# Scanning the next batch's first two rows between the matmuls of fc2, loading look-ahead tokens at row 84, and moving the softplus bias to ScalarE

## The reference

```python
xz = h @ in_w;  xs, z = split(xz);  xs = silu(xs)
proj = xs @ xproj_w
dt = softplus(proj[..., :512] + dt_bias)
Bm, Cm = ...                                # 64 states each
hst = hst * exp(dt_t * A) + (dt_t * x_t) * B_t     # 512 steps in time
y_t = einsum('bds,bs->bd', hst, C_t)
...
ffn_out = gelu(x2 @ fc1_w.T + fc1_b) @ fc2_w.T + fc2_b
x = x + ffn_out * gamma2
```

## Time and profile before

| | |
|---|---|
| median of 3 runs | 3171.84 us (3170.88 to 3175.58) |
| profiled execution | 3174.25 us, its span 3172.5 us |
| PE / DVE / ACT / POOL busy | 98% / 87% / 85% / 78% of the span |
| rows 0 to 127 of batch 1, from its first scan | 852.1 to about 1469 us |
| fc2 between batches 0 and 1 | 837.5 to 851.3 us |

### The profile page before, as it was taken

One profiled execution on the slowest core, in us unless ns is written; L12 is line 12 of the kernel. 1 busy time (PEld: TensorE's weight loads), 2 busy tenths in 40 slices (PEclk: granted clock), 3 DMA queues, 4 the chain that ended last, 5 costly groups with the idle time before them and its releaser, 6 DMA issues.

```text
span 3172.5 us, 59515 instructions
## 1 busy us (share of the span) xinstructions
PE 3097.2 (98%) x23304; PEld 2631.1 (83%) x23304; DVE 2759.5 (87%) x3049; ACT 2703.8 (85%) x4496; POOL 2484.2 (78%) x638
## 2 busy tenths in 40 slices
PE   8999999999999999999999999999999999999999
PEld 6998899884699889988479988998848998888965
DVE  3999999977499999997659999999666999999963
ACT  3999999974699999995579999999558999999845
POOL 2999999971199999996139999999415999999910
PEclk9999999999999999999999999999999999999999
DMA  5222222210222232221022232223102223222100
GB/s 185 80 84 67 85 73 84 74 56 29 74 69 82 74 92 68 82 85 65 1 84 67 82 87 79 74 82 89 46 14 80 81 76 89 69 74 82 57 14 8
DMA packets 195240, 225.69 MB, mean 71 GB/s; under 512 B 77449, under 2 KB 149641, under 8 KB 193681
## 3 DMA queue, kind: packets, MB, share of 16 engines
q1 hardware_dynamic: 194960, 221.89, 22.8%
HBM read 217.37 MB, written 4.48 MB: 70 GB/s over the span
## 4 chain that ended last, share of the span: by engine, by line
PE 82%; POOL 8%; issue 4%; DVE 3%; ACT 1%; DMA 0%; SPq 0%; DVEq 0%; ACTq 0%; POOLq 0%
PE bank L1129 23%; PE bank L1109 17%; PE bank L1009 11%; PE bank L1110 10%; POOL states L674 5%; PE bank L1105 4%; PE bank L1353 4%; POOL y_gated L674 3%; PE bank L1390 2%; PE bank L1493 2%; PE bank L1378 2%; DVE states L1640 2%; PE bank L1184 1%; PE bank L1136 1%; PE bank L1281 1%
## 5 line engine op out<-in xcount | busy, mean ns | idle before, releaser
L674 POOL TENSOR_TENSOR states<-states,c_rows 128x2048 f32<-128x2048 f32 x336 | 1531.6, 4574 | 132.4 <-DVE states L1640 129.9
L1640 DVE TENSOR_TENSOR_SCAN states<-decay,bank 128x512 f32<-128x512 f32 x1376 | 1577.4, 1201 | 16.5 <-ACT decay L854 1.2
L854 ACT ACTIVATE decay<-dt,a_log 128x512 f32<-128x512 f32 x2048 | 1305.5, 710 | 0.0
L845 ACT ACTIVATE inflow_tok<-dtx_tok,b_tok 128x512 f32<-128x512 f32 x1536 | 995.7, 713 | 85.7 <-PE bank L1110 74.6
L1109 PE MATMUL bank<-ident,inflow_tok 128*128 128x128 f32 x5280 | 904.7, 280 | 35.8 <-DVE states L1640 18.7
L1129 PE MATMUL bank<-ident,states 128*128 128x128 f32 x5504 | 826.0, 273 | 6.1 <-DVE y_gated L1646 3.0
L1640 DVE TENSOR_TENSOR_SCAN y_gated<-decay,bank 128x512 f32<-128x512 f32 x672 | 777.1, 1202 | 14.0 <-ACT decay L854 5.0
L674 POOL TENSOR_TENSOR y_gated<-y_gated,c_rows 128x2048 f32<-128x2048 f32 x168 | 768.4, 4574 | 19.8 <-DVE y_gated L1640 18.1
L1109 PEld LDWEIGHTS bank<-ident,inflow_tok 128*128 128x128 f32 x5280 | 598.9, 141 | 205.7 <-issue 87.6
L1110 PE MATMUL bank<-b_diag,dtx_tok 128*128 128x128 f32 x3520 | 681.3, 275 | 0.0
L1129 PEld LDWEIGHTS bank<-ident,states 128*128 128x128 f32 x5504 | 645.0, 141 | 14.3 <-POOL states L674 7.8
(11 more groups left out here) (174 smaller groups left out, 2592.3 us busy)
## 6 DMA issues: line engine op xcount, KB each, us to landing
c_rows<-c_spill SPq DMA_DIRECT2D x256, 512.0 KB, 3.7
b_diag<-diag_ring SPq DMA_DIRECT2D x256, 128.0 KB, 2.3
xproj_w<-in_xproj_w SPq DMA_DIRECT2D x32, 320.0 KB, 3.8
in_w<-in_in_w SPq DMA_DIRECT2D x16, 512.0 KB, 4.5
out_w<-in_out_w SPq DMA_DIRECT2D x4, 1024.0 KB, 8.2
in_w<-in_fc_w SPq DMA_DIRECT2D x8, 512.0 KB, 4.3
xproj_w<-in_w SPq DMA_DIRECT2D x8, 512.0 KB, 4.7
xproj_w<-in_fc_w SPq DMA_DIRECT2D x4, 1024.0 KB, 4.7
```

What stands on the lines that cost most here:

```text
L674: pool.tensor_tensor(state_row, state_row, c_row.to_broadcast([P, KI, L]), ALU.mult).then_inc(weighed, PAIRS)
L845: last_tok = act.activation(inflow_tok[:, r % SLOTS, t, :], dtx_tok[:, d, t, :], ACT.Copy, scale=b_tok[:, d, t, s:s + 1])
L854: act.activation(decay[:, r % SLOTS * KI + k, :], dt[:, d, k, :], ACT.Exp, scale=a_neg[:, d, k, s:s + 1]).then_inc(decay_ready, 1)
L1640: dve.tensor_tensor_scan(state_slots[r % STATES][:, k, time], decay[:, slot, time], banks[k % INFLOW_BANKS][:, time], 0.0, ALU.mult, ALU.a ...
```

## The change

Three edits in one. (1) PE interleaves ten turns of the next batch (rows 0 and 1, and two tiles of row 2) into fc2, after its matmuls number 9, 12, ... 31 (0 to 31); DVE scans rows 0 and 1 there, ahead of the residual adds of tiles 1, 2 and 3. In the row loop those turns and scans are left out for b > 0. SP loads `b_diag` of rows 2 and 3 right after the C rows of the next batch, before fc1 ends. (2) `x_ahead` of batch b+2 is loaded at row 84 of batch b, in place of batch b+1 at row 0; only batch 1's stays at row 0 of batch 0. (3) ACT adds the bias in place in the PSUM guest bank (Identity with bias), and takes Exp straight from the bank; DVE's two half caps go, and the cap of 40 moves into the last DVE step, which now is min and then max.

```diff
+EARLY_AT = (9, 12, 15, 18, 21, 24, 27, 30, 31, 31)
+EARLY_SCANS = SLOTS * KI
-DT_CAP = 30.0
+DT_CAP = 40.0
-DT_CAP_AT = (30, 36, 40, 44)
-DT_CAP_REST_AT = (31, 37, 41, 45)
+DT_BIAS_AT = (31, 37, 41, 45)
+AHEAD_LOAD_AT = 84
@@ SP, batch
-                    if d == 0 and at == 0 and not last:
-                        sp.dma_start(x_ahead[:], x_rows[b + 1]).then_inc(ahead_loaded, 16)
+                    if r == 0 and b == 0:
+                        sp.dma_start(x_ahead[:], x_rows[1]).then_inc(ahead_loaded, 16)
+                    if r == AHEAD_LOAD_AT and b + 2 < B:
+                        sp.wait_ge(ahead_norm, (b + 2) * TT)
+                        sp.dma_start(x_ahead[:], x_rows[b + 2]).then_inc(ahead_loaded, 16)
-                    if not (last and r == BATCH_ROWS - HALF):
+                    if (r or not b) and not (last and r == BATCH_ROWS - HALF):
                         load_diag(b * BATCH_ROWS + r + HALF)
...
                     spread_rows(b + 1, HALF)
+                    load_diag((b + 1) * BATCH_ROWS + HALF)
                     sp.wait_ge(fc1_mm, (b + 1) * KF)
@@ ACT, prepare
+                if s in DT_BIAS_AT:
+                    k = DT_BIAS_AT.index(s)
+                    if k == 0:
+                        act.preload_act_table_set("natural_log_exp_and_others")
+                    act.wait_ge(dt_mm, n * KI + k + 1)
+                    act.activation(guest[(k + 1) % 2], guest[(k + 1) % 2], ACT.Identity,
+                                   bias=dt_b[:, d, k:k + 1]).then_inc(dt_biased, 1)
                 if s in DT_EXP_AT:
                     k = DT_EXP_AT.index(s)
-                    if k == 0:
-                        act.preload_act_table_set("natural_log_exp_and_others")
-                    act.wait_ge(dt_capped, n * KI + k + 1)
-                    act.activation(part[:, k, :], part[:, k, :], ACT.Exp).then_inc(dt_exp, 1)
+                    act.wait_ge(dt_biased, n * KI + k + 1)
+                    act.activation(part[:, k, :], guest[(k + 1) % 2], ACT.Exp).then_inc(dt_exp, 1)
@@ PE, scan_row and fc2
-                    turn_inflow(b, r, k)
+                    if not b or r * KI + k >= len(EARLY_AT):
+                        turn_inflow(b, r, k)
...
+                        for i, at in enumerate(EARLY_AT):
+                            if at == t * KF + c and b < B - 1:
+                                turn_inflow(b + 1, i // KI, i % KI)
@@ DVE, prepare, batch
-                        last = dve.scalar_tensor_tensor(dt[:, d, k, c], guest[(k + 1) % 2][:, c], dt_b[:, d, k:k + 1],
-                                                        part[:, k, c], ALU.add, ALU.max)
+                        last = dve.scalar_tensor_tensor(dt[:, d, k, c], part[:, k, c], DT_CAP, guest[(k + 1) % 2][:, c],
+                                                        ALU.min, ALU.max)
-                    if s in (DT_CAP_AT[k], DT_CAP_REST_AT[k]):
-                        ...
-                        last = dve.tensor_scalar(part[:, k, c], guest[(k + 1) % 2][:, c], dt_b[:, d, k:k + 1], DT_CAP,
-                                                 ALU.add, ALU.min)
+            def early_scans(b, t, last):
+                for i in range(EARLY_SCANS):
+                    if EARLY_AT[i] // KF == t and not last:
+                        scan_row(b + 1, i // KI, (i % KI,))
+                    early = b > 0 and r * KI < EARLY_SCANS
+                    if not early:
+                        scan_row(b, r, range(0, PAIR))
...
                 for t in range(TT):
+                    early_scans(b, t, last)
                     dve.wait_ge(res_mm, (b * RES + 3) * TT + t + 1)
                     dve.tensor_tensor(x_out[:, t, :], banks[OUT_BANK + t][:, 0:D], x_att[:, t, :], ALU.add).then_inc(out_ready, 1)
```

More of the change, by code:

```diff
@@ L331, in build @@
         dt_mm = sem("dt_mm")
-        dt_capped = sem("dt_capped")
+        dt_biased = sem("dt_biased")
         dt_exp = sem("dt_exp")
@@ L859, in _ @@
             for s in range(NS):
-                if s == DT_EXP_AT[0]:
+                if s == DT_BIAS_AT[0]:
                     act.wait_ge(ssm_loaded, 16 * len(SSM))
@@ L1492, in batch @@
                             pe.wait_ge(fc1_ready, b * KF + c + 1)
-                        last = pe.matmul(banks[OUT_BANK + t][:, 0:D], gelu_h[:, c, t * P:(t + 1) * P], fc2_w[:, c, :],
-                                         start=(c == 0), stop=(c == KF - 1))
-                    last.then_inc(res_mm, 1)
+                        last_mm = pe.matmul(banks[OUT_BANK + t][:, 0:D], gelu_h[:, c, t * P:(t + 1) * P], fc2_w[:, c, :],
+                                            start=(c == 0), stop=(c == KF - 1))
+                        if c == KF - 1:
+                            last_mm.then_inc(res_mm, 1)
+                        for i, at in enumerate(EARLY_AT):
+                            if at == t * KF + c and b < B - 1:
+                                turn_inflow(b + 1, i // KI, i % KI)
             for b in range(B):
@@ L1599, in prepare @@
                             dve.wait_ge(dt_log, n * KI + k + 1)
-                        last = dve.scalar_tensor_tensor(dt[:, d, k, c], guest[(k + 1) % 2][:, c], dt_b[:, d, k:k + 1],
-                                                        part[:, k, c], ALU.add, ALU.max)
+                        last = dve.scalar_tensor_tensor(dt[:, d, k, c], part[:, k, c], DT_CAP, guest[(k + 1) % 2][:, c],
+                                                        ALU.min, ALU.max)
                         if s == DT_READY_REST_AT[k]:
                             last.then_inc(dt_ready, 1)
-                    if s in (DT_CAP_AT[k], DT_CAP_REST_AT[k]):
-                        c = part_of(s, DT_CAP_AT[k], DT_CAP_REST_AT[k])
-                        if s == DT_CAP_AT[k]:
-                            dve.wait_ge(dt_mm, n * KI + k + 1)
-                        last = dve.tensor_scalar(part[:, k, c], guest[(k + 1) % 2][:, c], dt_b[:, d, k:k + 1], DT_CAP,
-                                                 ALU.add, ALU.min)
-                        if s == DT_CAP_REST_AT[k]:
-                            last.then_inc(dt_capped, 1)
             def look_ahead(b, s):
@@ L1657, in _ @@
                     dve.tensor_scalar(scale_cap[:], scale_mul[:], MAX_SCALE_MUL, None, ALU.min).then_inc(cap_ready, 1)
-                if s == DT_CAP_AT[0]:
-                    dve.wait_ge(ssm_loaded, 16 * len(SSM))
                 if s == DT_READY_AT[0]:
@@ L1670, in batch @@
                     d, s = r // NS, r % NS
-                    scan_row(b, r, range(0, PAIR))
+                    early = b > 0 and r * KI < EARLY_SCANS
+                    if not early:
+                        scan_row(b, r, range(0, PAIR))
                     if d == 0 or not last:
@@ L1683, in batch @@
                         gate_rows(b, 0)
-                    scan_row(b, r, range(PAIR, KI))
+                    if not early:
+                        scan_row(b, r, range(PAIR, KI))
                 r = BATCH_ROWS - 1
```

## The result

The changed kernel takes **3157.98 us** in the median of 4 runs (3156.91 to 3159.10), the kernel before 3173.71 in the 4 runs beside them: ratio **0.9949, 95% interval 0.9935 to 0.9964**, so 15.7 us faster by the medians. The profiled executions differ by 17.3 us (3174.25 to 3156.91). The forecast was 3152.0 with 3143 to 3166 around it: the time lies 6.0 us above the forecast and inside the range. Of these, 1.9 lie in the kernel before, whose median came out at 3173.71 where the forecast started from 3171.84; the gain itself is 15.7 us where 19.8 were forecast.

The account below looks back on a forecast made before the run. Four nearly full engines bound the rows (POOL paces direction 0, DVE direction 1), with bubbles ahead of batches 1 to 3. Early scans and loads 14.8, softplus 4.5, first preparation 0.5: 19.8 us off 3171.84 gives 3152.0 us, range 3143 to 3166.

Parts of the forecast that it names:

- fc2 and the early turns: Next batch's turns and scans inside fc2: fc2 ends 4.4 us later, turns 1.85 us apart, POOL's row 2 earlier.
- the tenth turn's wait: At fc2's end, PE's tenth turn must wait for the eighth scan, to 857.2 us.
- the 16.3: Gains up to POOL's row 2 in batches 1 to 3: 5.9, 7.1 and 3.3 us, before the store's loss.
- The loads' share: Part of the gain up to row 2 from moved loads: 2.6 us in batch 1, 3.8 in batch 2.
- Rival 2: Early turns in fc2 gain nothing, fc2 stretching as much as scans gain; only loads' 6.4 us left, 3165.4 us; chance 0.08.
- The output store: ACT waits for it ahead of row 4; landing in 6.0 us, it loses 1.5 us over batches 1 to 3.
- The lead of 2.2: ACT's decay of row 5 ready 2.2 us before its scan in batch 1, absorbing part of the store wait.
- Softplus: Seven preparations in the row loops: DVE loses 3.0 us each, ACT gains 2.4; gain 4.5 us, bounds 9 gained, 3 lost.
- The start: First preparation, ahead of batch 0's rows: shorter chains and an earlier table load, 0.5 us gained.
- the signs that would have made the prediction wrong: fc2 growing by more than 5 us, rows losing pace behind row 4, or DVE waiting for decay in softplus rows.
- Rival 1: ACT sets the first rows, row 4 waiting for the store: 8.6 us gained, softplus nothing, 3162.7 us; chance 0.17.
- Rivals 3 and 4: In softplus preparations: 3, ACT becomes the bound, 3180.3 us, chance 0.07; 4, Identity reloads tables, about 3240 us, chance 0.02.

Follow-up runs that it names:

- e5: Only the two load edits (x_ahead at row 84, b_diag of rows 2 and 3 before fc1's end) on the kernel before: 3168.75 us, ratio 0.9986.
- e1: The changed kernel with ACT's wait for the output store moved from ahead of row 4 to ahead of row 10: 3149.28 us, ratio 0.9921.
- e8: The changed kernel with one more ACT copy of 512 columns behind each softplus Identity: 3158.62 us, single run.
- e7: The changed kernel with two added DVE instructions of 256 columns per tile, both inputs in SBUF, in all preparations but the first: 3317.55 us, single run.
- e12: The changed kernel with DVE's removed softplus load put back behind the select, reading a PSUM bank and constants: 3166.63 us, ratio 0.9978.
- e4: The softplus edit alone on the kernel before: 3161.49 us, ratio 0.9960.
- e10: The changed kernel with the store wait at row 10 and the ten early turns spread more evenly over fc2: 3150.72 us, ratio 0.9927.
- e11: The changed kernel with the 512 KB load of x_in issued at row 10 in place of row 2: 3152.62 us, single run.
- e2: The changed kernel with SP issuing the output store ahead of the four xproj_w loads: 3150.43 us, ratio 0.9926.
- e9: The changed kernel with two more ACT copies of 512 columns behind each softplus Identity: 3167.21 us, single run.

## Why the prediction was right, and where not

1. **fc2 and the early turns: right.** fc2 18.4 us long (forecast 18.2), turns 1.85 apart, the eighth scan and the tenth turn's wait where they were put. POOL's row 2 came 25.4 us after fc2's first matmul in all three batches (861.08 - 835.67, and 25.4 twice more) against 25.0 forecast, so 5.5, 6.7 and 2.9 = 15.1 us of the 16.3. The table's marks show 16.5, since attention and MLP were 1.4 us shorter in this execution. The loads' share of it, 2.6 + 3.8, was 2.4 + 3.6 when done alone (e5, with the caution given there). Rival 2 is out.
2. **The output store: the mechanism was right, the size was not; this is the step that failed.** The sum had a landing of 6.0 us, read from one batch, and came to a loss of 1.5. The store was issued 20.2 us after fc2's first matmul, as worked out, but landed 7.6, 7.3 and 7.5 us later. Put into the same formula, 7.6 in batch 1 lets ACT move 1.5 in place of 3.1 and gives 5.9 - 1.5 - 2.2 = 2.2 us lost (measured 2.2); batches 2 and 3 give 1.7 and 2.0 (measured 1.7 and 2.3), the 2.0 with the 0.4 that the forecast's 1.5 kept for batch 3's lead. In sum 5.9 against 6.1 measured. The lead of 2.2 was about right. e1 shows the cause: without the wait there, 5.7 of the 6.1 are back. I had kept the landing as a single value, though it stood directly on the path; the trace of before already had 6.9 in batch 2.
3. **Softplus: too small, for a wrong reason.** 8.2 us against 4.5. I let ACT's 2.4 us bound direction 1 to 1.3 of its 2.8 us; the twenty rows gained 1.7, 1.8 and 1.4 us in batches 0 to 2. ACT had more room than its idle time in the window says: the lead that the forecast would not draw on took up the work, and e8 put 2.5 us more into it at no cost. Batch 3's direction 0 gave 1.4 (0.6 taken), and the direction 0 preparations that I put at nothing, with the rows around all of them, 1.8 in sum. Identity's 650 ns is less than the 687 of the nearest row, and Exp from the bank takes 589 where it took 628 from SBUF (L810 before); e8 says that this didn't matter. The Trainium skill (ScalarE: Activation LUTs, "Step-by-step: what each stage is for") has a ScalarE output to PSUM quicker than one to SBUF. The trace agrees as far as two different functions can show it: the Identity into the bank takes 650 ns, the gelu into SBUF 687.
4. **The start: can't be read.** 0.5 us was forecast; POOL's first row came 1.0 later. PE no longer waits for dt inside the projection as in the earlier trace rows, but the spread of the start hides a part of this size (last section).
5. **Sum.** Forecast 14.8 + 4.5 + 0.5 = 19.8; by the same terms 15.1 - 6.1 + 8.2 = 17.2, with the 1.4 and the -1.0 of the stages around them 17.6. The store's error of 4.6 us and softplus' 3.7 point in opposite directions: that the time comes as near to the forecast as it does is in part luck. Of the signs that would have made the prediction wrong none came: fc2 grew by 4.4 us, behind row 4 the rows keep their 4.8 us, and DVE has no wait for decay in the twenty rows of direction 1. Rival 1 had half of it: row 4 waits for the store, but softplus didn't give nothing. Rivals 3 and 4 are out: Identity loads no table, and ACT isn't the bound until two more instructions a tile are added.

## What to carry to other kernels

When work is moved ahead of a transfer, list who waits for that transfer and take its landing time as a range over all its places, not one row: here 1.5 us of it, three times, was most of the miss. A wait for a store belongs at the first write that reuses its source, and a store that somebody waits for goes ahead of the loads that nobody does. Idle time of an engine in a window is not its room: what it can take was found only by adding work to it until the time moved. And before a loss in one execution is put down to an edit, its clock is read.

## What the chip showed that I had not expected

**Two SBUF inputs on DVE beside POOL.** 2738 ns in place of 398 for 256 columns, while POOL's own instructions kept their 4575 ns (4577 in the kernel after). The trace of e7 shows that this is a wait and not slower work:

```profile
2184.06 4.55 POOL L681 TENSOR_TENSOR states<-states,c_rows 128x2048 f32<-128x2048 f32 x1
...
2186.22 2.68 DVE L1614 SCALAR_TENSOR_TENSOR scratch<-xs 128x256 f32<-128x256 f32 x1
...
2191.31 4.54 POOL L681 TENSOR_TENSOR states<-states,c_rows 128x2048 f32<-128x2048 f32 x1 [2.69 <-DVE states L1651]
```

POOL's instruction ends at 2188.61 and DVE's at 2188.90, 0.29 us later. All 56 are like this: each ends 0.28 to 0.29 us after the end of a POOL instruction, so they take 1.5 us where little of POOL's was left and, once, 5.0 us, where POOL had started its next one first. Then POOL stands 2.69 us for scans that DVE couldn't start, and both engines lose. The kernel before holds the comparison already (duration in ns, least, median, greatest):

```profile
L1690 DVE TENSOR_TENSOR states<-states,c_rows x8: 676/1598/3201, 687.5 to 3008.0; 128x512 f32<-128x512 f32 x8
L1716 DVE TENSOR_TENSOR decay<-inflow_tok,b_diag x16: 691/691/693, 735.0 to 3058.3; 128x512 f32<-128x512 f32 x16
```

Both have two SBUF inputs of 512 columns. The sixteen of L1716 run in the attention, with POOL idle, and take 691 ns. Of L1690 four run with POOL idle, 676 to 680 ns, and four start beside POOL's last instructions of a batch, 2515 to 3201 ns. L1699, with one input in PSUM, takes 692. So two SBUF inputs cost nothing by themselves; a POOL instruction under way does. The Trainium skill (GPSIMD Engine Reference, "1. Specifications") names the cause that fits: the SBUF interfaces are shared, and an instruction of VectorE with two SBUF inputs contends for them. The trace agrees and gives a price. In e12, whose second input is a constant and whose first is in PSUM, the pieces ran at 417 ns beside the same POOL work.

**PE's clock at the start.** From 66 to 74 us, shortly before the first rows, the windows show (columns as in the earlier trace rows) for the kernel before, after, and e1:

```profile
66.00:74.00 8.00, 7.68 (x26) 3.21 (x26) 2.91 (x6) 7.55 (x13) 0.00 (x0) 0.77 0.01 3
```

```profile
66.00:74.00 8.00, 8.00 (x24) 2.96 (x24) 1.93 (x5) 7.46 (x13) 0.00 (x0) 0.64 0.02 6
```

```profile
66.00:74.00 8.00, 7.28 (x36) 3.76 (x34) 5.65 (x6) 8.00 (x14) 0.00 (x0) 1.00 0.37 93
```

The granted clock is partly at its 1.2 GHz level in the first two and at 2.4 GHz throughout in the third, with PE about as busy. It had fallen in all three between 58 and 66, and in the third it was back sooner: from 62 to 66 it was 0.50, 0.50 and 0.76, after 4 us (58 to 62) in which PE was busy for 1.8, 1.1 and 2.0. From 66 to 74 it was 1.00 too in e4, e5, e10 and e11, and 0.55 to 0.70 in e2, e7, e8, e9 and e12; the first group has its first row 1.5 to 3.2 us earlier than the kernel before, the second 0.2 to 3.1 us later (table, start; e7, which isn't in it, 0.2). e1 differs from the kernel after in nothing that lies ahead of these rows, and starts 4.0 us earlier, so this is between executions and not the edits'. Why the clock comes back sooner in some isn't settled. The difference at the start is as large as what several of these experiments look for, and the reason that they are judged by stretches of rows rather than by the whole time.
